# Filler matmuls on TensorE during its waits ahead of the first projections and, in the last batch, ahead of the turns of x1 and of h

## The reference

```python
def layer0(x, adj):                       # 8 heads of 16
    q, k, v = x @ Wq, x @ Wk, x @ Wv
    scores = where(adj > 0, q k^T / 4, -1e9)       # per head, 1024 x 1024
    return softmax(scores) v @ Wo + bo
def layer1(x, adj):
    h = x @ W.T
    e = (h @ a1)[:, None] + (h @ a2)[None, :]
    e = where(e >= 0, e, 0.2 * e)
    return softmax(where(adj > 0, e, -9e15)) @ h
x = layernorm(x + layer0(x, adj))
x = layernorm(x + layer1(x, adj))
```

## Time and profile before

| | before |
|---|---|
| median of three runs | 897.36 us (896.6 to 897.99) |
| the profiled execution | 896.19 us |
| its span, first to last instruction | 894.2 us |
| mean granted TensorE clock | 0.968 |
| TensorE, matmuls busy | 814.8 us, 91% of the span |
| VectorE busy | 698.0 us, 78% |
| ScalarE busy | 701.9 us, 78% |
| GpSimd busy | 118.2 us, 13% |

### The profile page before, as it was taken

How to read it: one execution, slowest core, us unless ns; L and a number is a source line. 1 busy time by engine, 2 the same in 40 slices (tenths; PEclk the granted TensorE clock), 3 DMA queues, 4 the chain that set the end, 5 groups by cost and what they waited for, 6 DMA issues and landing times.

```text
span 894.2 us, 19419 instructions
## 1 busy us (share of the span) xinstructions
PE 814.8 (91%) x7597; PEld 398.1 (45%) x7629; DVE 698.0 (78%) x1141; ACT 701.9 (78%) x766; POOL 118.2 (13%) x92
## 2 busy tenths in 40 slices
PE   6299989999999999999999999999999999999681
PEld 3123334334643366334643357334654357434671
DVE  4188779797788977988788977988788987787563
ACT  1299898999679986899779986899769996897050
POOL 4000100030003020031002120122000220122030
PEclk8589999999999999999999999999999999999986
DMA  4647716551266125451365224561364323401001
GB/s 138 151 127 185 152 48 173 150 118 48 83 170 153 48 82 136 130 128 60 107 160 150 47 72 144 152 132 48 113 151 138 63 84 87 92 2 49 1 13 37
DMA packets 51778, 92.14 MB, mean 103 GB/s; under 512 B 3729, under 2 KB 20882, under 8 KB 51666
## 3 DMA queue, kind: packets, MB, share of 16 engines
q1 hardware_dynamic: 51682, 90.85, 39.0%
HBM read 67.63 MB, written 23.20 MB: 102 GB/s over the span
## 4 chain that ended last, share of the span: by engine, by line
PE 67%; ACT 16%; issue 10%; DVE 5%; DMA 0%; POOL 0%; ACTq 0%; POOLq 0%; SPq 0%; DVEq 0%
PE acc L474 17%; ACT weights L619 12%; PE slot L509 12%; PE slot L441 9%; PE slot L450 9%; PE slot L520 3%; PE slot L446 3%; PE slot L453 2%; ACT atts L645 2%; PE slot L557 2%; DVE x L907 2%; PE slot L575 2%; PE slot L567 2%; PE slot L547 2%; PE slot L491 1%
## 5 line engine op out<-in xcount | busy, mean ns | idle before, releaser
L619 ACT ACTIVATE weights<-slot 128x1024 f32<-128x1024 f32 x504 | 491.7, 1041 | 77.3 <-PE slot L450 39.4
L831 DVE SCALAR_TENSOR_TENSOR weights<-mask,weights 128x1024 f32<-128x1024 bf16 x336 | 403.4, 1235 | 53.7 <-ACT weights L619 43.4
L474 PE MATMUL acc<-weights,vst 128*17 128x512 f32 x2048 | 243.3, 593 | 0.0
L441 PE MATMUL slot<-qst,kst 97*32 97x512 bf16 x2240 | 160.5, 383 | 5.8 <-ACT weights L619 5.2
L450 PE MATMUL slot<-qst,kst 97*128 97x512 bf16 x464 | 133.6, 388 | 27.2 <-issue 15.4
L509 PEld LDWEIGHTS slot<-hst,atts 128*128 128x128 f32 x896 | 106.8, 191 | 17.4 <-ACT weights L619 9.6
L509 PE MATMUL slot<-hst,atts 128*128 128x129 f32 x896 | 110.5, 276 | 3.2 <-issue 1.7
L474 PEld LDWEIGHTS acc<-weights,vst 128*17 128x17 f32 x2048 | 52.3, 97 | 119.5 <-issue 96.8
L441 PEld LDWEIGHTS slot<-qst,kst 97*32 97x32 bf16 x2240 | 49.6, 95 | 115.8 <-ACT weights L619 49.3
L846 DVE SCALAR_TENSOR_TENSOR atts<-turn,hst,mask 128x1024 f32<-128x1024 f32 x64 | 83.0, 1321 | 23.2 <-DMA k_scratch<-atts 15.5
L768 POOL TENSOR_TENSOR rstd<-vareps,exponent 128x4 f32<-128x4 f32 (+1 forms) x24 | 29.3, 1221 | 467.0 <-DVE vareps L902 467.0
(11 more groups left out here) (131 smaller groups left out, 676.7 us busy)
## 6 DMA issues: line engine op xcount, KB each, us to landing
raw<-in_adjT SPq DMA_DIRECT2D x64, 512.0 KB, 3.8
q_scratch<-atts SPq DMA_DIRECT2D x48, 256.0 KB
qst<-q_scratch SPq DMA_DIRECT2D x16, 768.0 KB
k_scratch<-atts SPq DMA_DIRECT2D x24, 256.0 KB
kst<-k_scratch SPq DMA_DIRECT2D x16, 384.0 KB
xT_sb<-in_xT SPq DMA_DIRECT2D x8, 512.0 KB, 4.8
kst<-k_scratch SPq DMA_DIRECT2D x16, 256.0 KB
x_sb<-in_x SPq DMA_DIRECT2D x8, 512.0 KB, 4.7
```

The lines of the kernel that those rows point to most:

```text
L441: mm = pe.matmul(ps[rows, cols], kst[:, h, keys], qst[:, h, cols], start=True, stop=not by_pe)
L474: mm = pe.matmul(acc[VW * i:VW * i + HD + 1, cols], vst[b % 2][:, t, g * HG + i], weights[:, HG * buffer(b, n) + i, cols], start=(t == 0), ...
L619: act.activation(to, ps[:], ACT.Exp, scale=SCALE).then_inc(exp_done, 1)
L831: dve.scalar_tensor_tensor(out=to, in0=masks[b % 2][:, n % T], scalar=0.0, in1=at, op0=ALU.is_equal, op1=ALU.mult).then_inc(masked, 1)
```

## The change

Three groups of products are put into TensorE's program whose results nobody reads; each writes where the next real product writes over it.

Nine of 128 columns in float32, `ones` by `ones` into `acc`, at the head of TensorE's program, once GpSimd has set `pool_step` for the first time. In the last batch, 28 of 512 columns in bfloat16, `same` by a mask tile into x1T's slot, ahead of its wait for `x1_made`, and five more into h0's slot, ahead of its wait for `taken["x1T"]`.

```diff
                 elif name == "x1T":
+                    if me == B - 1:
+                        keep_busy(ps, 28)
                     pe.wait_ge(x1_made, me + 1)
                     for t in range(T):
                         mm = pe.transpose(ps[:, t * 128:(t + 1) * 128], x1[me % 2][:, t], ident[:])
                 elif name in ("h0", "h1"):
+                    if me == B - 1 and name == "h0":
+                        keep_busy(ps, 5)
                     pe.wait_ge(taken["x1T"], me + 1)
...
+            def keep_busy(to, times):
+
+                for _ in range(times):
+                    pe.matmul(to[:, 0:HALF], same[:], masks[(B - 1) % 2][:, 0, 0:HALF], **kw)
+
+            pe.wait_ge(pool_step, 1)
+            for _ in range(9):
+                pe.matmul(acc[:, 0:128], ones[:], ones[:], **kw)
 
             for b in range(-1, B + 2):
```

## The result

The changed kernel takes 890.86 us as a median of five executions (889.27 to 891.81), the kernel before 896.6 in the same comparison (894.03 to 897.99): ratio 0.9936, 95% interval 0.9914 to 0.9959. It is faster by 0.6%. Two later comparisons of the same change gave 0.9942 (0.9925 to 0.9960) and 0.9947 (0.9930 to 0.9964). Over all runs of this study the change has a mean of 891.1 us (27 executions), the kernel before 896.1 (111 executions, standard deviation 1.8): 5.0 us, with an uncertainty of 0.7 (two standard errors). The forecast of 893.1 was 2.2 us too high, and 890.86 lies 0.3 us under its range of 891.2 to 896.0.

The account below looks back on a forecast made before the run. TensorE's low clock after waits, on the chain at the start and in the last batch, was taken as the bound. Gains of 3.1 and 1.2 us, together 4.3, off the median of 897.36 gave 893.1 us, range 891.2 to 896.0.

Parts of the forecast that it names:

- The base: The kernel before's median of 897.36 us, 1.2 above its profiled execution, from which the gain was subtracted to give 893.1.
- The start: Nine products ahead of q raise the clock earlier, so q and the first unit come 1.2 us earlier.
- the bound of 1.7: Upper bound in us of the gain on q, if the clock is full before q starts.
- Nothing is gained or lost there: After k the clock falls as before, so `fold_second_layer` and the first units stay at 0.50: no gain or loss.
- The end: In the last batch x1T, h0 and fi run at full clock, saving 0.85, 0.91 and 1.36 us, together 3.1.
- I add nothing for it: A clock fall in the wait ahead of L491, possible in some executions of either kernel, counted as nothing.
- B: The clock's rise at the start comes no earlier, so the start gives nothing: 894.3 us, chance 0.14.
- C: The clock falls behind the 28; x1T gains 0.85 us, h0 and fi nothing: 895.3 or 896.2 us, chance 0.14.
- D: The added products do not count for the clock, nothing changes: 898.3 us, or 897.4 with the start's 1.2; chance 0.06.
- E: The 28 run over and delay x1T by 4.8 us at the low clock: slower, 901.9 us, chance 0.04.
- A: The forecast itself: start and last batch both gain, 893.1 us, own range 891.4 to 894.6, chance 0.62.

Follow-up runs that it names:

- experiments 10 and 11: The change plus 16 products between k and `fold_second_layer` and 12 ahead of L491 (889.87, 888.64 us); 11 adds 64 ahead of the first unit (890.09 us).
- one-column end: The change with the 28 and the five products of the last batch at one column instead of 512: 895.9 us against 896.47, ratio 0.9994.
- the nine on top of fold fillers: The kernel before plus the nine and sixteen products between k and `fold_second_layer`, none in the last batch: 892.93 us, ratio 0.9976.
- change again: The change itself, unaltered, timed once more beside the kernel before: 891.05 us against 896.58.
- experiment 8: The change without the nine at the start, plus twelve products in the wait ahead of L491: 891.04 us, ratio 0.9946.
- experiment 5: The kernel before plus only the 28 products ahead of x1T, without the nine and the five: 891.92 us, ratio 0.9952.
- experiment 6: The change without the nine at the start and with 48 products instead of 28 ahead of x1T: 895.66 us, ratio 0.9990.
- experiment 4: The change without the nine at the start, only the 28 and the five of the last batch: 892.88 us, ratio 0.9958.

## Why the prediction missed

The direction and both mechanisms were right, the number was 2.2 us too high. Of these, 1.2 are the base, 0.7 the gain, and the rest is where the first five executions happened to fall (890.86 against a mean of 891.1). The 0.2 are luck, and they count: the mean of 891.1 lies only 0.1 under the range.

**The base: the step that failed first.** "Against the median of 897.36, which stands 1.2 above it, it is 893.1". Three executions were taken for the kernel before, and the 1.2 us between them and the profiled one for something real. 111 executions have a mean of 896.1, which is where the profiled one stood (896.19); the same sum from there gives 891.8. The 111 run from 892.0 to 900.1; three of them say their mean no better than to 1.0 us (1.8 over the root of three). The range had to hold that, and it let the base vary only down to the profiled run, together with the largest start.

**The start, forecast 1.2: right for q.** q's parts leave at 14.0 us in the mean of the six traces without the nine (13.88 to 14.14) and at 12.7 in that of the eight in the table with them (12.45 to 13.10): 1.3 us, and 1.2 if the three of experiments 10 and 11 are counted (12.48 to 13.30). In no trace was it nothing, and in none more than the bound of 1.7. The first unit starts at 39.5 us in the mean of the six and at 38.2 in that of the eight: 1.3 us, with a standard error of 0.6. What the start is worth in time, I can only put together from pieces: 1.5 us in the spans with nine and with eight, and with ten 0.8 us of time lost while the program's end took 2.5 us longer than before's, so some 1.7 gained; 0.9 with the one-column end; the change against the end alone 1.5; the nine on top of fold fillers 1.3; each with 0.6 to 0.8. Their mean is 1.4. The first three leave out what the program's end took, and no single comparison of times shows the start's gain beyond the noise.

**"Nothing is gained or lost there": wrong as a description.** I had `fold_second_layer` at the low clock in both kernels, since the trace showed it so. The table has 7.1 to 9.9 us from q's to k's parts, with no filler of its own in the fold: the clock may hold, fall and rise again, or fall and stay low, and the trace of before (9.91) was the slowest of fourteen. At the wait behind k I wrote that it "lets the clock fall as surely as before": in two traces without a filler there it did not fall at all. Of the 3.8 us by which the changed kernel's first unit led in the profile, 1.07 are q's, 1.15 came this way, and the remaining 1.6 in the transfers, whose length changed from trace to trace (15.6 to 18.9 us from k's parts to the first unit). The last two are not shown to be a gain of the change: "change again" has 9.60 and a first unit at 39.48, the end alone without any filler there 8.62 and 40.01. Without fillers in the fold, q's to k's parts take 8.3 us in the mean of the five traces without the nine and 9.0 in that of the seven with them, so nothing is gained there. So the profile after looks better than the change is.

**The end, forecast 3.1: right.** 0.85, 0.91 and 1.36 came out to a hundredth, the 28 were hidden with 1.1 us to spare (I had 1.2), the copy was not held up by the five. Where the clock did not fall ahead of L491, x1T to last is 37.0 without end fillers (three traces) and 33.8 with: 3.2. Measured with the start left out it is 3.5 and 4.1, each with 0.6. Over all traces of the table, with or without the fall ahead of L491, the means of x1T to last are 38.3 without end fillers and 34.8 with: 3.5, with a standard error of 0.8.

**"I add nothing for it": the term put at nothing.** By the traces the two ends are worth 3.2 and 1.3 us, 0.2 more than the 4.3 forecast. The other 0.5 of the 5.0 stays open and is not clear of the noise (0.3 is the standard error of the 5.0 alone). The term that I put at nothing and that the traces show not to be nothing is the wait ahead of L491. From L491's start to VectorE's last instruction it is 24.7 us where the clock held and 26.2 to 27.5 where it fell, so the fall costs 1.5 to 2.9 us. It shows in four of seven traces without the fillers of the last batch and in two of six with them and without products ahead of L491. That the change makes this fall rarer or cheaper, and so gains the 0.5, is not shown by so few. What is shown is that the fall is there to be had: with twelve products in that wait it is gone, x1T to last is 33.8 in each trace, and the standard deviation of the times shrinks to a third (experiment 8). The reason I gave for the median standing above the profiled run was this fall. It does make executions scatter, as the fold does, but the 1.2 us that it was to explain were not there.

**The rivals.** B (the start gives nothing) fits the times of three kernels with the start alone, but not their traces: q was done earlier in each, and in each the end of the program took 1.3 to 2.7 us longer than in the mean of the others. C (the clock falls around x1T) is refuted where it was tried, even without the five (one trace). The Trainium skill, page "TensorE: Matmul & The Clock Gate", Part 4: PE-mode transpose, had spoken for C. The granted clock of 1.00 through x1T, h0 and fi in the trace of experiment 5 shows that 1.1 us of transposes between two gaps of 1.1 and 1.3 us did not bring it down; whether transposes count less than other products, this does not tell. D is refuted by the granted clock. E's mechanism exists: 20 products more are 4.3 us, 1.1 of them still fit into the wait, x1T comes 3.2 us late, and by experiment 6 against experiment 4 this costs 2.3 us with a standard error of 0.8. The change's 28 don't run over.

**Slips that changed nothing.** D's second figure should be 897.1 (898.3 less 1.2), not 897.4. The range "takes A's lower edge" but starts at 891.2 where A's is 891.4; 890.86 is under both. The page's row is under nine tenths in the first three slices, not in two and a half.

What stays open: what in the program's end takes 9.6 to 10.3 us in some kernels and 11.3 to 12.7 in the three with the start alone. The one-column end, with the change's number of instructions and nearly the work of the start alone, has 9.8, which speaks for the make-up of the program and against what runs; one kernel does not settle it. Whether it is the fetching of instructions behind the last jump was not tried.

## What to carry to other kernels

A wait of TensorE on the path that sets the end costs twice, once as a wait and once as the low clock of what follows it; products that fill it for nothing were free here as long as they ended before the wait did, and beyond that cost about their overrun (3.2 us late, 2.3 with 0.8 measured). Price what follows the wait by the same jobs where they stand amid other work in the same trace, and look for every wait on that path: each one left uncovered is a loss in some executions and a scatter in the measurement. And before a change of half a per cent is forecast or judged, know how far executions of the same kernel lie apart: here a base of three was off by as much as one of the two gains, and the one profiled execution of the change stood 1.8 us under its mean.

## What the runs showed of the hardware

The granted clock of TensorE falls at other places in each execution of one and the same kernel: behind k's end it held through a wait of 3.5 us in two kernels that had no filler there (7.08 us from q's to k's parts; "end without the five" and "end and ahead of L491"), fell at 11 to 16 us and came back 3 to 7 us later in others, and stayed low for ten microseconds in the trace of before. The first of the two:

```profile
14.34 1.96 PE L586 MATMUL acc<-turn,ident 128*128 128x512 f32 x4 [3.48 <-DVE turn L1012]
```

Ahead of L491 a wait of 2.85 us was harmless in seven traces; waits of 2.5 to 2.9 us ended at the low clock in six others, which cost 1.5 to 2.9 us.

With 28 products of one column (0.84 us) at the head of the wait ahead of x1T, x1T ran at the low clock (1.97 us); with 28 of 512 columns (6.0 us) it ran at the full one (1.09).

A program's end, behind the last instruction of its work, was 1.3 to 2.7 us longer than the mean of the other fourteen traces (10.0) in three kernels that differ from the kernel before by 16 to 20 of 7,600 matmul records. In one of them the profile shows it inside the span, in two outside.
